# Projecting tiles of x inside the attention instead of in a stage ahead of it

## What is computed

```python
xn = layernorm(x)                       # x: 4 x 1024 x 512, no learned weights
c_Q  = rms_norm(xn @ Wq_down) * q_norm_w          # 192 wide
c_KV = rms_norm(xn @ Wkv_down) * kv_norm_w        # 128 wide
k_pe = rope(rms_norm(xn @ Wk_pe) * k_pe_norm_w)   # 64 wide, shared by all heads
q_nop, q_pe = c_Q @ Wq_up, rope(c_Q @ Wq_pe)      # 16 heads of 128 and of 64
k_nop, v = split(c_KV @ Wkv_up)                   # 8 key/value heads of 128, each used by 2 heads
attn = softmax(causal([q_nop, q_pe] @ [k_nop, k_pe].T / sqrt(192)))
y = (attn @ v) @ Wo
ffn = ternary(xn, 0.33, 0.5) @ (ternary(weight, 0.2, 0.6) + rram).T
out = x + y + ffn
```

## Time and profile before

| | |
|---|---|
| median of 3 runs | 1915.51 us (1914.29 to 1915.68) |
| time of the profiled execution | 1908.69 us |
| its span, first to last instruction | 1906.9 us |
| mean granted TensorE clock | 0.974 |

### The profile page before, as it was taken

One profiled execution on the slowest core, in us unless ns is written; L12 is line 12 of the kernel. 1 busy time (PEld: TensorE's weight loads), 2 busy tenths in 40 slices (PEclk: granted clock), 3 DMA queues, 4 the chain that ended last, 5 costly groups with the idle time before them and its releaser, 6 DMA issues.

```text
span 1906.9 us, 29505 instructions
## 1 busy us (share of the span) xinstructions
PE 1741.3 (91%) x9190; PEld 895.3 (47%) x9190; DVE 1291.0 (68%) x3182; ACT 1129.0 (59%) x2379; POOL 423.6 (22%) x1042
## 2 busy tenths in 40 slices
PE   2767766999999999999999999999999999999997
PEld 1333333454455554444554544545545455554453
DVE  6557774767677767667676767576777776776664
ACT  3765664656565656556565656565666656655554
POOL 2334462112111122111212121212121112111121
PEclk9888886999999999999999999999999999999999
DMA  5988853787977786969787758888878777778774
GB/s 171 249 216 203 227 152 71 137 152 144 166 137 146 135 149 120 173 123 162 142 153 139 146 112 162 149 149 157 149 141 135 143 141 140 143 143 149 140 138 86
DMA packets 934747, 285.78 MB, mean 150 GB/s; under 512 B 904000, under 2 KB 908352, under 8 KB 934400
## 3 DMA queue, kind: packets, MB, share of 16 engines
q1 hardware_dynamic: 915184, 257.85, 70.9%
q10 hardware_dynamic: 19408, 26.06, 4.6%
HBM read 37.91 MB, written 23.07 MB: 32 GB/s over the span
## 4 chain that ended last, share of the span: by engine, by line
PE 75%; DMA 7%; DVE 7%; issue 4%; ACT 3%; POOL 1%; SPq 1%; ACTq 0%; DVEq 0%; POOLq 0%
PE bank L418 6%; PE bank L422 6%; PE bank L419 6%; PE bank L421 6%; PE bank L420 6%; PE bank L439 6%; PE bank L441 6%; PE bank L440 6%; PE bank L454 5%; PE bank L453 5%; PE bank L452 5%; DMA FT<-F 3%; DMA X<-in_x 2%; PE bank L386 2%; PE bank L388 1%
## 5 line engine op out<-in xcount | busy, mean ns | idle before, releaser
L717 ACT ACTIVATE P<-P,nm 128x256 f32<-128x256 f32 (+7 forms) x512 | 396.6, 775 | 619.9 <-DVE nm L1041 619.7
L1041 DVE CUSTOM_DVE_ANT_0 P<-bank,mask,neg 128x256 f32<-128x256 f32 (+7 forms) x512 | 417.4, 815 | 426.8 <-PE bank L422 426.6
L1054 DVE SCALAR_TENSOR_TENSOR F<-P,rc,F 128x256 f16<-128x256 f32 (+7 forms) x512 | 410.8, 802 | 0.8 <-ACT F L699 0.6
L699 ACT ACTIVATE F<-P,rc 128x256 f16<-128x256 f32 (+7 forms) x512 | 389.8, 761 | 12.9 <-DVE rc L1049 11.4
L1169 POOL TENSOR_SCALAR sn<-sm 128x1 f32<-128x1 f32 x512 | 138.7, 271 | 661.2 <-ACT P L717 659.7
L418 PE MATMUL bank<-KQ,Q 128*128 128x512 f16 (+3 forms) x768 | 250.9, 327 | 8.7 <-DMA Q<-QS 5.2
L419 PE MATMUL bank<-KQ,Q 128*128 128x512 f16 (+3 forms) x768 | 250.8, 327 | 0.0
L421 PE MATMUL bank<-KQ,Q 128*128 128x512 f16 (+3 forms) x768 | 250.8, 327 | 0.0
L422 PE MATMUL bank<-KQ,Q 128*128 128x512 f16 (+3 forms) x768 | 250.8, 327 | 0.0
L420 PE MATMUL bank<-KQ,Q 128*128 128x512 f16 (+3 forms) x768 | 250.8, 327 | 0.0
L439 PE MATMUL bank<-FT,V 128*128 128x512 f16 x576 | 218.7, 380 | 15.2 <-DMA FT<-F 15.0
(11 more groups left out here) (173 smaller groups left out, 2594.0 us busy)
## 6 DMA issues: line engine op xcount, KB each, us to landing
X<-in_x SPq DMA_DIRECT2D x32, 256.0 KB, 4.6
oscr<-X SPq DMA_DIRECT2D x32, 256.0 KB, 2.8
RES<-oscr ACTq DMA_DIRECT2D x32, 256.0 KB, 3.3
FT<-F SPq DMA_TRANSPOSE x512, 3.7
out<-RES ACTq DMA_DIRECT2D x32, 256.0 KB, 3.3
cscr<-CC SPq DMA_DIRECT2D x24, 256.0 KB, 2.2
chunk<-in_Wo ACTq DMA_DIRECT2D x4, 1024.0 KB, 7.9
wo<-in_Wo SPq DMA_DIRECT2D x4, 1024.0 KB, 6.2
```

The source lines that it names most:

```text
L699: return e.eng.activation(dst, src, ACT.Copy, scale=scale)
L717: e.eng.activation(m.P[:, u % 4, 0:w], m.P[:, u % 4, 0:w], ACT.Exp, bias=m.nm[:, u % 8:u % 8 + 1], scale=-1.0, accum_out=m.sm[:, u % 8:u % ...
L1041: e.eng.tensor_tensor_reduce(out=m.P[:, u % 4, 0:w], in0=m.pS[u % 2][:, off:off + w], in1=m.mask[:, 1024 - w:1024], scale=m.neg[:, :], sca ...
L1054: e.eng.scalar_tensor_tensor(out=m.F[:, u % FSLOTS, w:2 * w], in0=m.P[:, u % 4, 0:w], scalar=m.rc[:, u % 8:u % 8 + 1], in1=m.F[:, u % FSLO ...
```

## The change

The projection stage is gone. Tiles 0 to 2 are projected in a prologue, and tile t + 3 is projected inside the four groups of tile t and the first of tile t + 1 (`LEAD = 3`). Query tiles are taken in rising order in all batches, since tile t then needs the keys of tiles up to t alone. Nothing is written to DRAM and read back: keys stay in K (2 batches), c_Q in C (2 tiles), and x + ffn stays in X until the attention's output is added to it and stored. All weights are loaded once, in the prologue, where they are squared and folded without pieces of tiles between them. A tile has single buffers for XS, XT, CR and CC. Square roots are now exp(-0.5 ln v), so that one activation table serves the whole kernel. The number of matmuls hardly changes. F has 4 places and the ring of FT 16, where they had 5 and 23.

```diff
-ORDER = (0, 7, 1, 6, 2, 5, 3, 4)
-ORDER_LAST = (3, 4, 2, 5, 6, 7, 1, 0)
-FSLOTS, RING, AHEAD = 5, 23, 2
+FSLOTS, RING, AHEAD = 4, 16, 2
+LEAD, XSLOTS, NF, NW = 3, 5, 4, 24
 # TensorE, attention, in the loop over groups n = 4 t + g and quarters q
+            if q == 1 and (g == 3 and t + LEAD < T or g == 0 and t and t + LEAD - 1 < T):
+                e.wait_ge(s.yl, n)
+                if g:
+                    tiles.down(t + LEAD, m.pY[(n + 1) % 2])
+                else:
+                    tiles.ffn(t + LEAD - 1, m.pY[(n + 1) % 2])
 # TensorE, end of the prologue
+    for n in range(2 * AHEAD):
+        queries.up_pe(n)
+        outputs(4 * n)
+        outputs(4 * n + 1)
+        queries.up(n)
+        outputs(4 * n + 2)
+        outputs(4 * n + 3)
 # ScalarE
+                if (g, q) == (1, 1):
+                    tiles.ln_root(t + LEAD)
+                elif (g, q) == (1, 3):
+                    tiles.norm(t + LEAD)
+                elif (g, q) == (2, 0):
+                    tiles.x_hi(t + LEAD)
+                elif (g, q) == (3, 2):
+                    tiles.down_out(t + LEAD, m.pY[(n + 1) % 2])
+                if (g, q) == (0, 0):
+                    tiles.squares(t + LEAD - 1)
+                    tiles.rms_root(t + LEAD - 1)
+                elif (g, q) == (0, 2):
+                    tiles.parts_hi(t + LEAD - 1)
 # VectorE
+                if (g, q) == (1, 0):
+                    tiles.stats(t + LEAD)
+                elif (g, q) == (1, 2):
+                    tiles.ln(t + LEAD)
+                elif (g, q) == (2, 1):
+                    tiles.x_signs(t + LEAD)
+                if (g, q) == (0, 1):
+                    tiles.rms(t + LEAD - 1)
+                elif (g, q) == (0, 2):
+                    tiles.ffn_out(t + LEAD - 1, m.pY[(n + 1) % 2])
+                elif (g, q) == (0, 3):
+                    tiles.parts_lo(t + LEAD - 1)
 # GpSimd: x_lo at (2, 0), rotate_keys at (1, 0), keys at (1, 3)
 # SyncE
-            if q == 1 and g % 2 and b + 1 < NB and n // NG % NT < 4:
-                turn_keys(b + 1, 2 * (n // NG % NT) + g // 2)
+            if (g, q) == (2, 2) and t + LEAD < T:
+                tiles.turn_x(t + LEAD)
+            if (g, q) == (2, 0) and t and t + LEAD - 1 < T:
+                tiles.keep(t + LEAD - 1)
+    def keep(self, t):
...
+        e.eng.dma_start_transpose(out=m.C[:, t % 2, :, :], ...)
+        e.eng.dma_start_transpose(out=m.K[:, :, at * 128:at * 128 + 128], ...)
+        e.eng.dma_start(m.V[:, at, :, :], m.CC[:, 1, :, 0:128]).then_inc(s.v_in, 16)
 # SyncE, prologue, after the loads of x, of the down and feed-forward weights and the tables
+    (ua, ub, ub, pa, pbw, pbw, kv)
+    tiles.turn_x(0)
+    load_x(2)
+    (wo in four parts)
+    load_x(3)
+    tiles.keep(0)
+    tiles.turn_x(1)
+    tiles.keep(1)
+    tiles.turn_x(2)
```

More of the change, by code:

```diff
@@ L68, in score_cuts, with key_slot @@
     return off, [(0, cut)] + ([(cut, w)] if w > cut else [])
[L71 to L81, removed]
+def key_slot(t):
+    return t // NT % 2 * NT + t % NT
 class Engine:
@@ L145, in __init__ @@
[L145 to L171, removed]
@@ new lines, in tensor_prologue @@
+    tiles.down(0, m.pY[0])
+    e.wait_ge(s.f_sq, 1)
+    sums(2, 3)
+    for c in range(4):
+        turn_f(c)
+    tiles.ffn(0, m.pY[1])
+    e.wait_ge(s.q_sq, 5)
+    sums(3, 8)
+    tiles.down(1, m.pY[0])
+    tiles.ffn(1, m.pY[1])
+    fold(0)
+    fold(1)
+    tiles.down(2, m.pY[0])
+    tiles.ffn(2, m.pY[1])
+    fold(2)
+    fold(3)
+    e.wait_ge(s.o_sq, 4)
+    sums(8, 12)
+    for n in range(2 * AHEAD):
[5 more added lines that the diff above has]
+        outputs(4 * n + 3)
@@ L406, in score, with tensor_attention @@
+def tensor_attention(e, m, s, tiles, queries):
     def score(n, h):
@@ L455, in combine @@
         op.then_inc(s.c, 1)
-    e.wait_ge(s.od, T)
-    e.wait_ge(s.cr, T)
-    e.wait_ge(s.wl, 8 * NG)
-    for n in range(2 * AHEAD):
-        up_pe(n)
-        up(n)
     for n in range(AHEAD):
@@ L697, in scalar_attention @@
-def scalar_attention(e, m, s, cscr, oscr, out):
+    e.wait_ge(s.tern, 4)
+    square(m.fr[:, :, :], 2, (s.f_sq, 1))
+    tiles.down_out(0, m.pY[0])
+    tiles.squares(0)
+    tiles.rms_root(0)
+    e.wait_ge(s.scale, 2)
+    for c in range(4):
+        e.wait_ge(s.ft, c + 1)
+        copy(m.wfh[:, c, :], fold_bank(m, c), m.fsc[:, :]).then_inc(s.wfh, 1)
+    tiles.parts_hi(0)
+    tiles.ln_root(1)
+    tiles.norm(1)
+    tiles.x_hi(1)
+    e.wait_ge(s.wqs, 1)
+    e.wait_ge(s.ld_ua, 48)
+    square(m.ua[:, :], 3, (s.q_sq, 1), scale=m.wq[:, 0:1])
@@ new lines, in scalar_prologue @@
+    square(m.ub[0:64, :], 4, (s.q_sq, 2), p=64, scale=m.wq[0:64, 1:2])
+    e.wait_ge(s.ld_pe, 48)
+    square(m.pa[:, :, :], 6, (s.q_sq, 3), scale=m.wq[:, 0:1])
+    square(m.pbw[0:64, :, :], 7, (s.q_sq, 4), p=64, scale=m.wq[0:64, 1:2])
+    e.wait_ge(s.kvs, 1)
+    square(m.kv[:, :, :], 5, (s.q_sq, 5))
+    tiles.down_out(1, m.pY[0])
+    tiles.squares(1)
+    tiles.rms_root(1)
+    tiles.parts_hi(1)
+    fold_out(0)
+    tiles.ln_root(2)
+    tiles.norm(2)
+    tiles.x_hi(2)
+    rotary_out()
@@ new lines, in scalar_prologue @@
+    fold_out(1)
+    tiles.down_out(2, m.pY[0])
+    tiles.squares(2)
+    tiles.rms_root(2)
+    for c in range(2):
+        e.wait_ge(s.ld_wo[c], 16)
+        square(m.wo[:, 4 * c:4 * c + 4, :], 8 + c, (s.o_sq, c + 1))
+    tiles.parts_hi(2)
+    fold_out(2)
+    for c in range(2, 4):
+        e.wait_ge(s.ld_wo[c], 16)
+        square(m.wo[:, 4 * c:4 * c + 4, :], 8 + c, (s.o_sq, c + 1))
+    fold_out(3)
+    e.wait_ge(s.wfl, 4)
+    e.wait_ge(s.wrl, 2)
+    e.wait_ge(s.o_sq, 4)
+    for n in range(2 * AHEAD):
+        queries.rotated_hi(n)
+        outputs_out(4 * n)
+        outputs_out(4 * n + 1)
+        queries.queries_hi(n)
+        outputs_out(4 * n + 2)
+        outputs_out(4 * n + 3)
@@ L1031, in maximum, with vector_attention @@
+def vector_attention(e, m, s, tiles, queries):
     def maximum(u):
```

1393 lines of the change are left out of this document (664 added, 729 removed).

## The result

The changed kernel takes 2041.45 us in the median of 4 runs (2032.26 to 2042.90), the kernel before 1914.90 beside it (4 runs, 1909.39 to 1915.68): a ratio of 1.0657, 95% interval 1.062 to 1.0695. It is 6.6% slower, where 1846 us and a faster kernel were forecast.

A forecast was written before the change was run, and what follows sets the result against it. TensorE was taken as the bound after the projection stage, SyncE's queue as the new limit. Attention 1599.4 + tiles 106.7 - 15 + prologue 146 = 1837.1 us of span, 1846 us as median against 1915.5; range 1815 to 1870.

The forecast's parts named there:

- The step that failed: SyncE's queue, tiles 5 to 7: turned F waits only for the group before last (ring holds two), so `down` costs nothing.
- the slower one: Rival, 8 in 100: XT late, `down` stops TensorE in every tile; gain gone at 2.4 us a tile, 2040 at worst.
- Stops of the narrow tiles and the queue: TensorE's stops in the attention: 7 + 5 = 12 us a batch against 15 before, 11 us less over 3.66 batches.
- The rival on this: Narrow tiles 0 and 1, GpSimd delaying VectorE by shared ports: 27 us, 1873; with the queue's upper bound 1897; 17 in 100.
- Tail and rising order: End of the attention on the widest tile: 10 us less; rising wide tiles cost nothing.
- Wide tiles: Attention's wide query tiles: no stops in rising order, VectorE's and ScalarE's added work hidden behind TensorE, room in SyncE's queue.
- Projections: 29 tiles projected in the attention at 3.68 us each: 106.7 us, all on TensorE's path.
- Prologue: Three tiles and the weights before the first score: 146 us, bounds 120 to 185.
- Clock: TensorE's clock stays low for longer at the start: 6 us added.
- The main forecast's upper end: Range of the main forecast, 1815 to 1870 us, given 58 in 100.
- the queue's bound of +24: SyncE's queue on narrow tiles: shortfall 3 to 13 us a batch, taken as 7, so -16 to +24 on the sum.
- half the prologue's: Half of the prologue's bounds, 120 to 185 us around 146, counted into the main forecast's range.

The follow-up runs named there:

- kernel 1: Changed kernel with groups of six or more key tiles placed at place 0 or 8 of the ring by turns: 1914.90 us, ratio 1.0029.
- 9: Kernel 8 with GpSimd's `x_lo` cut from 512 to 64 columns for the tiles in the attention: 1891.10 us, ratio 0.9906.
- 8: Kernel 1 with `keep` (two transposes and a copy of a tile's queries, keys and values) issued one group later in SyncE's queue: 1902.96 us, ratio 0.9964.
- 12: Kernel 8 with `x_lo` one quarter later and the statistics of x and the steps after them a quarter later: 1875.94 us, ratio 0.9823.
- 4: Kernel before with query tiles in rising order in all batches, its ring of 23 kept: 1920.41 us, ratio 1.0054.
- 5: Kernel 1 with only 2 of the 8 matmuls of `ffn` for the 29 tiles in the attention: 1884.51 us, ratio 0.9868.
- 6: Kernel 1 with GpSimd's `x_lo` one quarter later, behind the scaling of the sum: 1918.81 us, ratio 1.0049.
- 10: Kernel 8 with `x_lo` one quarter later, behind the scaling of the sum: 1893.38 us, ratio 0.9910.

## Why the prediction was wrong

It gave 1837.1 us of span and the trace has 2041.1, 204 more. Its terms, one by one:

- **The step that failed**: that turned F of tiles 5 to 7 waits for `weigh` of the group before last. It was taken from the size of the ring, and never from the places that the code hands out. In 12 groups it is the group just before, and that costs 129 us (kernel 1). This turns a kernel about level with the old into one 6.6% slower. None of the rivals was this mechanism. That the slower one ends at 2040 us for the latest landing in every tile, where 2041 was measured, is chance. It put the stops before `down`, for XT, in every tile; in fact they stand before the scores, in three groups a batch, and 2.4 us a tile at `down` was never reached: kernel 1 has 21 us of stops there, 0.7 a tile.
- **Stops of the narrow tiles and the queue**: 12 us a batch forecast; kernel 1 has 45.6, 33.5, 34.5 and 30.1. The sum has 12 x 3.66 = 44 us, kernel 1 143.6. The rival on this had the place in part, a part of the size (27 to 51 us more on the sum, where kernel 1's attention is 84 over it) and another cause: of the 70 us by which kernel 1 stops more than the kernel before, tiles 0 and 1, which it names, have 26; tiles 2 and 3 have 20 and tile 7 has 23. `x_lo` holds up GpSimd's own scaling of sums, some 12 us of it (9); `keep` stands in SyncE's queue, another 12 (8). With 12 they are 24 or 25 a batch after the first: the sum's own term was still half of what is there.
- **Tail and rising order**: -10 and "cost nothing" against +10 measured (4), 8 of it stops.
- **Wide tiles**: right for 5 and 6, 0.3 us of stops each in kernel 1. Tile 7 stops 7.7, since the narrow tile's F is due in it.
- **Projections**: 106.7 us, right as a count of columns at full clock. Left out in part, four fifths show (5).
- **Prologue**: 146 forecast, 136.9 measured. The first product was 1.5 us early, the query loop 5.4, and the loop took 26.3 us for a forecast of 30.
- **Clock**: +6 forecast. After the first score it is 0.99 in kernel 1 beside 1.00 before, and 0.96 in the changed kernel, where each large stop is followed by half clock.

With the ring's 129 us on top of 1837.1 the sum would be 1966; the other 75 are 84 of the stops, tail, order and clock less 9 of the prologue. The main forecast's upper end, 1870, has the queue's bound of +24 alone; half the prologue's, which it names too, would have made it 1890.

That the twelve waits, the place of `keep` and the place of `x_lo` are causes is shown by runs. That the order 7, 0 costs by two narrow groups behind the widest is argued from where the stops stand in 4, not tested apart. The 0.3% between kernel 1 and before is too near to the scatter of its own runs to be told in parts.

## What to carry to other kernels

When a ring or pool shrinks, write out its places for every step of the schedule, and look for steps that take the place of their direct predecessor: the number of places says only what could fit. In an engine that runs its queue in order, ask of each moved operation what stands behind it while it waits; a move can cost alone and pay together with the move of what it waits for, so try pairs. A full TensorE pays for most of the columns that move in, and the gain of a removed stage is its length less that price, before any stop is counted.

## What the runs showed of the hardware

- A stop of 7.5 us costs TensorE more than itself: the granted clock was 0.50 from 891.20 to 896.50, the 1.2 GHz level, before it was back at 1.00 (the stretch 903 to 910). All 12 large stops have such a half clock behind them in the trace. Some 2.65 of the 10.2 us are from that.
- A transposing DMA held SyncE about as long whatever it turned: 1.42 us for K of 128 x 512 and 1.41 for queries of 128 x 1536 (the rows of 8); in wide tiles the same queries took 1.67 (the row at 857.42). One transpose that is not ready delayed all behind it, those of queries in another buffer too: 27.13 us for the four at 859.18.
- GpSimd's scaling of a 128 x 1 sum, 288 ns in the mean of 512, took 0.64 us when it met VectorE's subtraction with two inputs in SBUF, and ended with it. `x_lo` took 1.16 us in kernel 8 and 1.60 in kernels 6, 10 and 12, where it meets that subtraction in every tile of the attention. Rows of the changed kernel, VectorE, GpSimd, and the group's mean:

```profile
648.02 1.09 DVE L853 SCALAR_TENSOR_TENSOR XS<-XN,XG 128x512 f16<-128x512 f32 x1
...
648.54 0.64 POOL L1252 TENSOR_SCALAR sn<-sm 128x1 f32<-128x1 f32 x1
```

```profile
L1252 POOL TENSOR_SCALAR sn<-sm 128x1 f32<-128x1 f32 x512 | 147.7, 288 | 466.3 <-ACT P L725 465.1 <-DVE rc L1097 0.9
```

The Trainium skill ("SBUF — State Buffer", section "SBUF: two separate sides") has the shared pair of ports held by one of the two engines for a whole instruction, and this row agrees: 648.54 + 0.64 is 649.18, 648.02 + 1.09 is 649.11. It was not what the stops before `up` in group 2 were made of (9).
